# Longer runs a partition for x and the down weights, slots in 32 registers, and the second tile's A asked for earlier

## The chip, the cores and the metric

The kernel runs on one NeuronCore of a Trainium2 chip. The metric is the device time of one execution in microseconds, taken as the median of several runs. The core has a TensorE (PE, matmuls), a VectorE (DVE), a ScalarE (ACT), a GpSimd (POOL) and a SyncE (SP), which here does nothing but wait and issue DMAs; 16 DMA engines carry what is issued.

## What is computed

All matrices are float32. x has 128 sequences of 32 tokens of width 512 (4096 tokens). Two blocks with residuals follow each other:

```python
x = x + ffn0(cond0(x))        # L0
x = x + ffn1(cond1(x))        # L1
# cond0: x @ W + b + 2 * (x @ A[slot]) @ B[slot]      one of 32 adapters of rank 16 for each sequence
# ffn0:  (silu(x @ Wg.T) * (x @ Wu.T)) @ Wd.T         width 1376
# cond1: x @ W.T + 2 * sum over the top 2 of 8 experts, gates from a router with a language bias
# ffn1:  x @ Wb.T + b + 2 * sum over the top 2 of 8 experts, gates normalised
```

## The kernel before

The tokens are cut into NT = 8 tiles of 512. Everything on TensorE is done with each number split into a high and a low part of type float32r and three products (high by high, low by high, high by low).

**Stage 1** is cond0 and runs over the tiles. TensorE's work for a tile t is: the base product, 4 output blocks m by 4 chunks k by 3 products (48 matmuls of 512 columns); after m = 1 the product x A (`lora_in`, 24 matmuls of 256 columns, two groups g of 8 sequences); last the product with B (`cond_lora`, 24 matmuls of 256 columns), which closes the four banks. ACT copies a closed bank into `c_out` (L1005), SP stores it in `c_scratch` (L756). For tile 0 the loop over k is the outer one.

ACT and DVE make the high and the low parts: of x (L977, L1418), of A (`a_hi` L988, `a_lo` L1430), of B (L993, L1433), of the masked x A (`lora_in`: `h_masked` L1443, `lh_hi` L999, `lh_lo` L1449). Both run in program order: for tile 0 they turn A, split half of x of tile 1 (`split_x(1, (0, 1))`), and only then do `lora_in(0)`. In the tiles that follow: A and B of tile t, then x of t + 1, then `lora_in(t)`, then the closings.

Beside that, stage 1 prepares the down weights. `load_down` brings four row blocks (two pairs) into `wd_raw`, POOL makes four sums of each group (`down_sums`), ACT and DVE split seven operands of each group into a ring of four `dt` buffers (`down_hi`, `down_lo`, spread over the tiles by `d_due`), and SP stores each in `wd_scratch` (L623) and the last one in `ws_scratch` (L618). The buffers of the down weights lie where later the operands `cop` of stage 2 lie. So ACT's first `cop_split`, which stands ahead of the closings of tile 6, waits for the store of `ws_scratch` to have landed.

A is fetched by `gather_a`: slots are read from SBUF into SP's registers by one `reg_load` (L552, a TENSOR_LOAD of 16 registers), and each of the 16 sequences of a tile costs a register instruction (L557) and a DMA of 32 KB (L558). There is one `a_raw` buffer, so the gathers of tile t + 1 wait for `a_lo` of tile t, group by group. B's rows come by an indirect DMA on POOL.

All of these DMAs but B's are issued by SP in one order written out by hand in `sync_program`: at the start x and w0 of tile 0 in parts, `gather_a(0)`, x of tile 1 in two halves, `load_down(0)`, `load_down(1)`; then in each turn t the load of x of t + 2 (which waits until x of tile t is split), `gather_a(t + 1)`, and the stores of tile t with the stores of the down weights between them. In turn 5 the first load of c (`load_c(0, 0)`) comes behind the gathers, in turn 7 the second (`load_c(0, 1)`), for which `cop_begin(0, 1)` waits on DVE ahead of `lora_in(7)`.

**Stage 2** (ffn0) goes over pairs of tiles with a Strassen-like scheme of seven products. Its weights pass through a ring of 12 slots `wring`: for the first pair of tiles they are made on the spot and stored, later they are loaded (L603) from `wgu_scratch` and `wd_scratch`, each load issued as soon as the slot 12 places back is free. A down slot is 6 matmuls. **Stage 3** is the second block, with the weights of cond1 and ffn1 folded.

The layouts in DRAM: x is (tile, chunk, partition, token), so a tile's chunk is 2 KB a partition and the chunks lie 256 KB apart; `w_down` is plain rows of 2 KB; `wd_scratch` is (pair, product, partition, 512), `ws_scratch` is (half, partition, 512).

Of the kernel before, what the change touches and what calls it, by code (L numbers as in the profile page):

```python
# [3 lines left out]
F32 = mybir.dt.float32  # L4
# [6 lines left out]
P = 128  # L11
TOK = 512
LANG_BIAS = 5.0
SCALING = 2.0
DMA = 16
# [13 lines left out]
def build(nc, x, slots, slot_list, langs, w0, b0, a_cols, b_rows, w_gate, w_up, w_down, wb1, rhs2, ra1, b2t, b1, out):  # L29
    NT, KC, _, _ = x.shape  # L30
    D = KC * P
    NF = w_gate.shape[0]
# [223 lines left out]

    c_dram = nc.dram_tensor("c_scratch", list(x.shape), F32, kind="Internal").ap()
    t_dram = nc.dram_tensor("t_scratch", [NS, 4, 2, P, TOK], F32, kind="Internal").ap()
    x2_dram = nc.dram_tensor("x2_scratch", list(x.shape), F32, kind="Internal").ap()
# [123 lines left out]
    def x_parts(t):  # L383

        return [[0], [1], [2, 3]] if t == 0 else [[0, 1], [2, 3]]

# [152 lines left out]
    def sync_program(e):  # L539
        def load_x(t, ks):  # L540
            if ks[0] == 0 and t >= 2:
                e.wait_ge(x_lo, nth(t - 2))
            part = slice(ks[0], ks[-1] + 1)
            e.dma_start(x_raw[t % 2][:, part, :], x[t, part].rearrange("k p f -> p k f")).then_inc(  # L544
                x_in[t % 2][ks[0]], DMA)

        slot_regs = [e.alloc_register(f"slot{n}") for n in range(NG * GB)]

        def gather_a(t):

            first = t * NG * GB
            e.reg_load(slot_regs, slot_sb[0:1, first:first + NG * GB])  # L552
            for g in range(NG):
                if t > 0:
                    e.wait_ge(a_lo_done, NG * (t - 1) + g + 1)
                for b in range(GB):
                    slot = e.snap(slot_regs[g * GB + b], min_val=0, max_val=a_cols.shape[0] - 1)  # L557
                    e.dma_start(a_raw[:, g, b, :], a_cols[bass.ds(slot, 1)].rearrange("s p c -> (s p) c")).then_inc(  # L558
                        a_in[g], DMA)
# [28 lines left out]
        def load_slot(n):  # L588
# [12 lines left out]
            src = {"g": wgu_dram[a, b] if kind == "g" else None, "d": wd_dram[b, a] if kind == "d" else None,  # L601
                   "s": ws_dram[a] if kind == "s" else None}[kind]
            e.dma_start(plain(wring[n % N_W][:, :]), src).then_inc(w_moved[n % N_W], DMA)  # L603

        def load_down(g):
            if g >= 2:
                e.wait_ge(dt_lo_done, d_turn[g - 2, 3] + 1)
            if g < n_groups:
                n = pairs_of(g)
                src = w_down[4 * g * P:(4 * g + 2 * n) * P, :].rearrange("(r k p) d -> p r k d", r=n, k=2)  # L610
                e.dma_start(wd_raw[g % 2][:, 0:n, :, :], src).then_inc(wd_in[g % 2], DMA)  # L611
            else:
                e.dma_start(wd_raw[g % 2][:, 0, 0, :], w_down[2 * NP * P:NF * P, :]).then_inc(wd_in[g % 2], DMA)

        def store_down(n):
            e.wait_ge(dt_lo_done, n + 1)
            if n == len(d_steps):
                e.dma_start(ws_dram.rearrange("b p f -> p b f"),  # L618
                            plain(dt_[n % 4][:, :, :, :]).rearrange("p b h c -> p b (h c)")).then_inc(ws_stored, DMA)
                return  # L620
            g, i = d_steps[n]
            c = pairs_of(g)
            e.dma_start(wd_dram[2 * g:2 * g + c, i].rearrange("r p f -> p r f"),  # L623
                        plain(dt_[n % 4][:, 0:c, :, :]).rearrange("p r h c -> p r (h c)")).then_inc(dt_stored[n % 4], DMA)

        def extras(s, pos):
# [3 lines left out]
            if pos == slot_at["d", 1, 0]:  # L630
                for mp in range(2):
# [7 lines left out]
                    e.dma_start(res[mp][:, :], x[2 * s, mp]).then_inc(res_in[mp], DMA)  # L639
                    e.dma_start(res[2 + mp][:, :], x[2 * s, 2 + mp]).then_inc(res_in[2 + mp], DMA)  # L640
            if pos == slot_at["d", 1, 1] and s == NS - 1:
# [6 lines left out]
            if pos == slot_at["d", 6, 0]:  # L648
                e.wait_ge(h10_lo_done, 2 * s + 2)
                for mp in range(2):  # L650
                    e.dma_start(s1[mp][:, :], x[2 * s + 1, 2 + mp]).then_inc(x_second_in[mp], DMA)
                    e.dma_start(s2[mp][:, :], x[2 * s + 1, mp]).then_inc(x_second_in[mp], DMA)
            if pos == slot_at["d", 6, 3] and s + 1 < NS:
# [1590 lines left out]
```

## Time and profile before

| | |
|---|---|
| median of 3 runs | 1008.69 us (1008.25 to 1009.37) |
| profiled execution | 1007.51 us, span 1005.8 us |
| mean granted TensorE clock | 0.993 |
| busy: PE, DVE, ACT, POOL | 98%, 59%, 46%, 25% |
| bytes moved | 230.15 MB, 229 GB/s over the span |

The profile is that of one execution. An engine is busy when it works on an instruction; the issuing of DMAs is not counted, and stands under SPq. "Idle before <- X" names what released the engine. The granted clock is a share of full speed, so that 0.5 is the lower of TensorE's two levels (1.2 GHz) and 1.00 the higher (2.4 GHz).

### The profile page before, as it was taken

To read this page: it belongs to the slowest core of one execution; us is meant where nothing else is said; L and a number is where in the kernel's file an instruction comes from. 1 tells how busy PE (TensorE), PEld (TensorE's weight loads), DVE (VectorE), ACT (ScalarE), POOL (GpSimd) and SP (SyncE) were. 2 spreads that over 40 slices of the span, in tenths; PEclk is the share of its full clock that TensorE was granted. 3 is DMA by queue.
4 is the path that set the end of the run, shared out by engine and by line. 5 is a ranking of instruction groups with operands and counts; after the bars stand their busy time and mean duration, and the time that the engine had idled before them with its cause. 6 is when DMAs were issued, how large, how long until landed. Compare 5 with 4: busy or idle time off the path is not lost.

```text
span 1005.8 us, 14263 instructions
## 1 busy us (share of the span) xinstructions
PE 982.6 (98%) x4723; PEld 828.9 (82%) x4723; DVE 591.6 (59%) x969; ACT 465.0 (46%) x854; POOL 254.6 (25%) x244
## 2 busy tenths in 40 slices
PE   8989988999999999999999999999999999999998
PEld 7778876888888888888888888888888899898986
DVE  5555457667697342389243279533358588785862
ACT  4544555556483333375233367133347265445342
POOL 4232104454420441330171140062131280000000
PEclk9999999999999999999999999999999999999999
DMA  7888767677777986787887687797679660606132
GB/s 256 266 285 275 243 211 282 215 271 245 253 269 259 317 279 194 210 293 234 298 288 195 192 278 266 241 306 231 193 221 378 213 217 22 240 33 230 63 106 84
DMA packets 138515, 230.15 MB, mean 229 GB/s; under 512 B 30789, under 2 KB 30790, under 8 KB 138186
## 3 DMA queue, kind: packets, MB, share of 16 engines
q1 hardware_dynamic: 136928, 225.01, 67.5%
q0 software_dynamic: 1376, 4.22, 1.2%
q8 instruction: 39, 0.64, 0.3%
q14 instruction: 34, 0.28, 0.1%
q10 hardware_dynamic: 138, 0.01, 0.0%
HBM read 165.74 MB, written 63.44 MB: 228 GB/s over the span
## 4 chain that ended last, share of the span: by engine, by line
PE 83%; SPq 12%; issue 2%; DVE 2%; DMA 1%; ACT 0%; ACTq 0%; DVEq 0%
PE bank L1855 82%; SPq L558 5%; SPq L552 1%; SPq L623 1%; SPq L756 1%; SPq L544 1%; PE bank L2008 1%; SPq L557 1%; DMA c<-c_scratch 1%; DVE xa_lo L1418 0%; DMA a_raw<-in_a_cols 0%; DMA slot_i<-in_slots 0%; DVE b_lo L1433 0%; SPq L611 0%; DVE hg L1677 0%
## 5 line engine op out<-in xcount | busy, mean ns | idle before, releaser
L1855 PE MATMUL bank<-cop_hi,wring 128*128 128x512 f32 x1234 | 380.7, 389 | 0.1
L1855 PEld LDWEIGHTS bank<-cop_hi,wring 128*128 128x128 f32 x1234 | 231.6, 188 | 48.6 <-ACT bank L1073 0.4
L1855 PE MATMUL bank<-cop_lo,wring 128*128 128x512 f32 x616 | 239.6, 389 | 0.0
L1855 PE MATMUL bank<-op_hi,wring 128*128 128x512 f32 x560 | 173.7, 389 | 0.0
L1505 DVE TENSOR_TENSOR v<-bank,p7s 128x512 f32<-128x512 f32 x44 | 30.4, 692 | 203.5 <-PE bank L1855 203.5
L1855 PEld LDWEIGHTS bank<-cop_lo,wring 128*128 128x128 f32 x616 | 115.6, 188 | 23.9
L1855 PEld LDWEIGHTS bank<-op_hi,wring 128*128 128x128 f32 x560 | 105.1, 188 | 21.8
L1855 PE MATMUL bank<-op_lo,wring 128*128 128x512 f32 x280 | 108.9, 389 | 0.0
L1104 ACT ACTIVATE s<-bank 128x512 f32<-128x512 f32 x44 | 26.3, 598 | 118.8 <-PE bank L1855 118.6
L1491 DVE TENSOR_TENSOR op_lo<-h,op_hi 128x512 fp32r<-128x512 f32 x100 | 72.8, 746 | 3.3 <-ACT op_hi L1061 3.1
L1061 ACT ACTIVATE op_hi<-h 128x512 fp32r<-128x512 f32 x100 | 62.8, 628 | 13.7 <-PE bank L1855 12.8
L854 POOL TENSOR_TENSOR h_t<-h,h 128x512 f32<-128x512 f32 x20 | 26.3, 1317 | 161.4 <-DVE h L1527 161.4
L1073 ACT ACTIVATE bank<-bank 128x512 f32<-128x512 f32 x44 | 25.6, 582 | 78.6 <-PE bank L1855 78.6
L1855 PEld LDWEIGHTS bank<-op_lo,wring 128*128 128x128 f32 x280 | 52.6, 188 | 10.9
L1855 PE MATMUL bank<-xa_hi,w_hi 128*128 128x512 f32 x128 | 52.4, 409 | 4.6 <-ACT c_out L1005 3.7
L893 POOL TENSOR_TENSOR t_sum<-x_second,x_second 128x256 f32<-128x256 f32 x12 | 9.4, 817 | 177.0 <-DMA x_second<-x_scratch 177.0
L1855 PE MATMUL bank<-xa_lo,w_hi 128*128 128x512 f32 x128 | 51.7, 404 | 0.0
L1855 PE MATMUL bank<-xa_hi,w_lo 128*128 128x512 f32 x128 | 51.3, 401 | 0.0
L1510 DVE TENSOR_TENSOR p7s<-bank,p7s 128x512 f32<-128x512 f32 x44 | 30.4, 692 | 25.0 <-PE bank L1855 24.9
L809 POOL DMA_INDIRECT b_raw<-in_b_rows,row_i x16 | 19.0, 1187 | 90.5 <-DVE b_lo L1433 84.1
L1080 ACT ACTIVATE p7s<-bank 128x512 f32<-128x512 f32 x44 | 26.3, 598 | 30.6 <-PE bank L1855 30.6
L1095 ACT ACTIVATE s<-bank 128x512 f32<-128x512 f32 x44 | 26.3, 598 | 30.6 <-PE bank L1855 30.6
(225 smaller groups left out, 1930.5 us busy)
## 6 DMA issues: line engine op xcount, KB each, us to landing
wring<-wgu_scratch SPq DMA_DIRECT2D x231, 256.0 KB, 3.0
wring<-wd_scratch SPq DMA_DIRECT2D x140, 256.0 KB, 4.9
wgu_scratch<-wring SPq DMA_DIRECT2D x77, 256.0 KB, 3.5
c_scratch<-c_out SPq DMA_DIRECT2D x32, 256.0 KB
c<-c_scratch SPq DMA_DIRECT2D x32, 256.0 KB, 3.2
xs_raw<-x_scratch SPq DMA_DIRECT2D x16, 512.0 KB, 5.8
out<-res SPq DMA_DIRECT2D x32, 256.0 KB, 2.1
x_raw<-in_x SPq DMA_DIRECT2D x15, 512.0 KB, 6.6
```

The source lines that it names most:

```text
L558: e.dma_start(a_raw[:, g, b, :], a_cols[bass.ds(slot, 1)].rearrange("s p c -> (s p) c")).then_inc(a_in[g], DMA)
L809: e.indirect_dma_start(out=b_raw[g][:, :], out_offset=None, in_=b_rows, in_offset=bass.IndirectOffsetOnAxis(ap=row_i[:, col:col + 1], axis=0),
L854: e.tensor_tensor(h_t3[p][:, :], h22[p][:, :], h12[p][:, :], ALU.subtract).then_inc(t3_done, 1)
L1061: e.activation(op_hi[n % N_OP][:, :], op_source[i][p][:, :], ACT.Copy).then_inc(op_hi_done, 1)
L1073: e.activation(bank_y[b][:, :], bank_a[b][:, :], ACT.Copy).then_inc(ay_done, 1)
L1080: e.activation(p7s[b][:, :], bank_w[b][:, :], ACT.Copy).then_inc(p7s_done, 1)
L1095: e.activation(s1[j % 2][:, :], bank_a[j % 2][:, :], ACT.Silu).then_inc(silu1_done, 1)
L1104: e.activation(s2[j % 2][:, :], bank_z[j % 2][:, :], ACT.Silu).then_inc(silu2_done, 1)
L1491: e.tensor_tensor(op_lo[n % N_OP][:, :], op_source[i][p][:, :], plain(op_hi[n % N_OP][:, :]), ALU.subtract).then_inc(op_lo_done, 1)
L1505: e.tensor_tensor(v[b][:, :], bank_z[b][:, :], p7s[b][:, :], ALU.add).then_inc(gc22_done, 1)
L1510: e.tensor_tensor(p7s[b][:, :], bank_y[b][:, :], p7s[b][:, :], ALU.add).then_inc(gc21_done, 1)
L1855: return e.matmul(out_ap, lhs, rhs, start=start, stop=stop, skip_group_check=True)
```

## The change

Three things are changed, all of them on the side of the DMAs; TensorE, VectorE, ScalarE and GpSimd run the same instructions in the same order.

1. **Layouts.** x becomes (tile, partition, chunk, token), so a whole tile is 8 KB a partition in one run. A tile's load is one DMA of 1 MB for t > 0 (`x_parts`), where there were two of 512 KB; for tile 0 the parts stay, and the last of them has a run of 4 KB. A user of one chunk of x now reads runs of 2 KB that lie 8 KB apart. The down weights are laid out by partition, so that the load of a group has a run of 8 KB (4 KB for the last pair). `wd_scratch` is (group, product, partition, pair, 512): a store writes runs of 4 KB, and a ring slot's load reads runs of 2 KB that lie 4 KB apart. `ws_scratch` likewise.
2. **Slots.** `reg_load` reads 32 registers for two tiles at even t and nothing at odd t.
3. **Order.** `gather_a(1)` is asked for ahead of `load_down(1)` and the load of x of tile 2.

```diff
-    NT, KC, _, _ = x.shape
+    NT, _, KC, _ = x.shape
...
-    wd_dram = nc.dram_tensor("wd_scratch", [NP, 8, P, 4 * P], F32, kind="Internal").ap()
-    ws_dram = nc.dram_tensor("ws_scratch", [2, P, 4 * P], F32, kind="Internal").ap()
+    wd_dram = nc.dram_tensor("wd_scratch", [(NP + 1) // 2, 8, P, 2, 4 * P], F32, kind="Internal").ap()
+    ws_dram = nc.dram_tensor("ws_scratch", [P, 2, 4 * P], F32, kind="Internal").ap()
...
-        return [[0], [1], [2, 3]] if t == 0 else [[0, 1], [2, 3]]
+        return [[0], [1], [2, 3]] if t == 0 else [[0, 1, 2, 3]]
...
-            e.dma_start(x_raw[t % 2][:, part, :], x[t, part].rearrange("k p f -> p k f")).then_inc(
-                x_in[t % 2][ks[0]], DMA)
+            e.dma_start(x_raw[t % 2][:, part, :], x[t][:, part, :]).then_inc(x_in[t % 2][ks[0]], DMA)
...
-        slot_regs = [e.alloc_register(f"slot{n}") for n in range(NG * GB)]
+        slot_regs = [e.alloc_register(f"slot{n}") for n in range(2 * NG * GB)]
...
-            first = t * NG * GB
-            e.reg_load(slot_regs, slot_sb[0:1, first:first + NG * GB])
+            n = NG * GB
+            if t % 2 == 0:
+                e.reg_load(slot_regs, slot_sb[0:1, t * n:(t + 2) * n])
...
-                src = w_down[4 * g * P:(4 * g + 2 * n) * P, :].rearrange("(r k p) d -> p r k d", r=n, k=2)
+                src = w_down[:, 4 * g:4 * g + 2 * n, :].rearrange("p (r k) d -> p r k d", r=n)
...
         load_down(0)
-        load_down(1)
         for t in range(NT):
+            if t == 0:
+                gather_a(t + 1)
+                load_down(1)
             if t + 2 < NT:
                 for ks in x_parts(t + 2):
                     load_x(t + 2, ks)
-            if t + 1 < NT:
+            if 0 < t < NT - 1:
                 gather_a(t + 1)
```

The change on SP, behind the last gather of tile 0. `x_raw_75` is the buffer of tile 1's x, `x_raw_74` that of tile 0 and then 2. Before:

```order
L558 DMA a_raw<-in_a_cols 128x64
L544 DMA x_raw_75<-in_x 128x2x512 x2
L611 DMA wd_raw_76<-in_w_down 128x4x512
L611 DMA wd_raw_77<-in_w_down 128x4x512
L544 DMA x_raw_74<-in_x 128x2x512 x2
L552 TENSOR_LOAD slot_sb
L557 ISA
L558 DMA a_raw<-in_a_cols 128x64
```

Now, with the middle of the 16 gathers of tile 1 left out:

```order
L559 DMA a_raw<-in_a_cols 128x64
L545 DMA x_raw_75<-in_x 128x2048
L612 DMA wd_raw_76<-in_w_down 128x2048
L558 ISA
L559 DMA a_raw<-in_a_cols 128x64
...
L559 DMA a_raw<-in_a_cols 128x64
L612 DMA wd_raw_77<-in_w_down 128x2048
L545 DMA x_raw_74<-in_x 128x2048
L759 DMA c_scratch<-c_out_50 128x512
```

The gathers of tile 1 have moved ahead of the second group of down weights and of tile 2's x, their TENSOR_LOAD is gone, and each tile of x is one DMA.

The change on SP between the stores of tile 1 and the gathers of tile 3, where `dt` are the split down weights. Before:

```order
L623 DMA wd_scratch<-dt_83 128x2x512
L756 DMA c_scratch<-c_out_53 128x512
L623 DMA wd_scratch<-dt_84 128x2x512
L611 DMA wd_raw_76<-in_w_down 128x2x512
L544 DMA x_raw_74<-in_x 128x2x512 x2
L552 TENSOR_LOAD slot_sb
L557 ISA
L558 DMA a_raw<-in_a_cols 128x64
```

Now:

```order
L624 DMA wd_scratch<-dt_83 128x1024
L759 DMA c_scratch<-c_out_53 128x512
L624 DMA wd_scratch<-dt_84 128x1024
L612 DMA wd_raw_76<-in_w_down 128x1024
L545 DMA x_raw_74<-in_x 128x2048
L558 ISA
L559 DMA a_raw<-in_a_cols 128x64
```

The stores and loads are the same in number but for x, with longer runs, and the TENSOR_LOAD is there in every second turn only.

## Rows read from the trace of the kernel before

**Rows 1.** Windows: busy us of each engine, granted clock, DMA share, GB/s
```profile
0.00:171.00 171.00, 151.42 (x789) 129.43 (x789) 95.32 (x138) 84.28 (x155) 50.21 (x56) 0.96 0.78 260
171.00:1006.00 835.00, 831.14 (x3935) 699.45 (x3934) 496.23 (x832) 380.75 (x700) 204.42 (x188) 1.00 0.67 222
```

**Rows 2.** Waits of PE, 20 to 172 us: total us, times, longest
```profile
PE bank L1855 <- DVE a_lo L1430: 6.8, 5, 2.2
PE bank L1855 <- DVE lh_lo L1449: 6.0, 3, 4.6
PE bank L1855 <- ACT c_out L1005: 3.7, 1, 3.7
```

**Rows 3.** Timeline of PE: start us, us, form, idle before and its releaser
```profile
22.88 0.39 PE L1855 MATMUL bank<-lh_hi,b_hi 128*128 128x256 f32 x1 [0.45 <-DVE lh_lo L1449]
...
25.85 0.40 PE L1855 MATMUL bank<-xa_hi,w_hi 128*128 128x512 f32 x1
...
33.60 0.39 PE L1855 MATMUL bank<-xa_hi,a_hi 128*128 128x256 f32 x1 [2.12 <-DVE a_lo L1430]
...
122.74 0.40 PE L1855 MATMUL bank<-xa_hi,w_hi 128*128 128x512 f32 x1
...
139.54 0.28 PE L1855 MATMUL bank<-lh_hi,b_lo 128*128 128x256 f32 x1
...
168.23 0.39 PE L1855 MATMUL bank<-cop_hi,wring 128*128 128x512 f32 x1
```

**Rows 4.** Windows behind two long waits of PE, columns as in rows 1
```profile
34.00:37.50 3.50, 3.50 (x19) 3.50 (x19) 3.12 (x6) 3.47 (x7) 1.24 (x2) 0.53 1.02 382
...
163.70:167.20 3.50, 3.43 (x16) 3.43 (x17) 3.29 (x6) 3.02 (x6) 1.15 (x2) 0.53 0.30 114
```

**Rows 5.** Timeline of SP: start us, us spent issuing, count
```profile
14.65 0.94 SPq L544 DMA_DIRECT2D x_raw<-in_x  x2
15.63 1.02 SPq L611 DMA_DIRECT2D wd_raw<-in_w_down  x2
16.70 1.98 SPq L544 DMA_DIRECT2D x_raw<-in_x  x2
19.88 12.07 SPq L558 DMA_DIRECT2D a_raw<-in_a_cols  x16
...
41.33 9.12 SPq L558 DMA_DIRECT2D a_raw<-in_a_cols  x16
...
138.78 8.57 SPq L558 DMA_DIRECT2D a_raw<-in_a_cols  x16
```

**Rows 6.** The loads of the slots: count, ns min/median/max, first and last start
```profile
L552 SPq TENSOR_LOAD <-slot_sb x8: 985/1547/3057, 5.0 to 135.5; - x8
```

**Rows 7.** A piece of the chain that ended last: start us, us
```profile
154.57 5.55 DMA c<-c_scratch
```

**Rows 8.** Windows: two neighbouring stretches of stage 1
```profile
52.00:66.00 14.00, 13.07 (x81) 11.47 (x80) 9.71 (x12) 7.87 (x15) 7.97 (x6) 1.00 1.02 367
66.00:72.00 6.00, 5.62 (x30) 4.41 (x28) 1.84 (x3) 1.47 (x3) 0.00 (x0) 1.00 0.33 74
```

**Rows 9.** Window of stage 2 in which rhs2 and wb1 (runs of 10 KB) land
```profile
755.00:760.00 5.00, 5.00 (x24) 4.14 (x23) 5.00 (x6) 2.98 (x6) 2.16 (x2) 1.00 1.01 422
```

**Rows 10.** Timeline of ACT: two idle times and what ended them
```profile
18.87 1.16 ACT L977 ACTIVATE xa_hi<-x_raw 128x512 fp32r<-128x512 f32 x2 [1.11 <-DMA x_raw<-in_x]
...
140.74 1.67 ACT L1046 ACTIVATE cop_hi<-c 128x512 fp32r<-128x512 f32 x3 [6.09 <-DMA ws_scratch<-dt]
```

**Rows 11.** DMA issues of the whole span: count, KB each, median us to landing
```profile
wring<-wd_scratch SPq DMA_DIRECT2D x140, 256.0 KB, 4.9
...
a_raw<-in_a_cols SPq DMA_DIRECT2D x128, 32.0 KB, 2.0
...
x_raw<-in_x SPq DMA_DIRECT2D x2, 256.0 KB, 3.7
w_raw<-in_w SPq DMA_DIRECT2D x2, 256.0 KB, 4.2
```

More of the change, by code:

```diff
@@ L255, in build @@
     bank_a, bank_y, bank_w, bank_z = (banks[i::4] for i in range(4))
-    c_dram = nc.dram_tensor("c_scratch", list(x.shape), F32, kind="Internal").ap()
+    c_dram = nc.dram_tensor("c_scratch", [NT, KC, P, TOK], F32, kind="Internal").ap()
     t_dram = nc.dram_tensor("t_scratch", [NS, 4, 2, P, TOK], F32, kind="Internal").ap()
-    x2_dram = nc.dram_tensor("x2_scratch", list(x.shape), F32, kind="Internal").ap()
+    x2_dram = nc.dram_tensor("x2_scratch", [NT, KC, P, TOK], F32, kind="Internal").ap()
     wgu_dram = nc.dram_tensor("wgu_scratch", [NF, 8, P, 4 * P], F32, kind="Internal").ap()
-    wd_dram = nc.dram_tensor("wd_scratch", [NP, 8, P, 4 * P], F32, kind="Internal").ap()
-    ws_dram = nc.dram_tensor("ws_scratch", [2, P, 4 * P], F32, kind="Internal").ap()
+    wd_dram = nc.dram_tensor("wd_scratch", [(NP + 1) // 2, 8, P, 2, 4 * P], F32, kind="Internal").ap()
+    ws_dram = nc.dram_tensor("ws_scratch", [P, 2, 4 * P], F32, kind="Internal").ap()
     sem = nc.alloc_semaphore
@@ L556, in gather_a @@
                 for b in range(GB):
-                    slot = e.snap(slot_regs[g * GB + b], min_val=0, max_val=a_cols.shape[0] - 1)
+                    slot = e.snap(slot_regs[(t % 2) * n + g * GB + b], min_val=0, max_val=a_cols.shape[0] - 1)
                     e.dma_start(a_raw[:, g, b, :], a_cols[bass.ds(slot, 1)].rearrange("s p c -> (s p) c")).then_inc(
@@ L600, in load_slot @@
                     e.wait_ge(w_moved[k % N_W], DMA * w_moves(k))
-            src = {"g": wgu_dram[a, b] if kind == "g" else None, "d": wd_dram[b, a] if kind == "d" else None,
-                   "s": ws_dram[a] if kind == "s" else None}[kind]
+            src = {"g": wgu_dram[a, b] if kind == "g" else None, "d": wd_dram[b // 2, a][:, b % 2, :] if kind == "d" else None,
+                   "s": ws_dram[:, a, :] if kind == "s" else None}[kind]
             e.dma_start(plain(wring[n % N_W][:, :]), src).then_inc(w_moved[n % N_W], DMA)
@@ L609, in load_down @@
                 n = pairs_of(g)
-                src = w_down[4 * g * P:(4 * g + 2 * n) * P, :].rearrange("(r k p) d -> p r k d", r=n, k=2)
+                src = w_down[:, 4 * g:4 * g + 2 * n, :].rearrange("p (r k) d -> p r k d", r=n)
                 e.dma_start(wd_raw[g % 2][:, 0:n, :, :], src).then_inc(wd_in[g % 2], DMA)
             else:
-                e.dma_start(wd_raw[g % 2][:, 0, 0, :], w_down[2 * NP * P:NF * P, :]).then_inc(wd_in[g % 2], DMA)
+                e.dma_start(wd_raw[g % 2][:, 0, 0, :], w_down[:, 2 * NP, :]).then_inc(wd_in[g % 2], DMA)
         def store_down(n):
@@ L617, in store_down @@
             if n == len(d_steps):
-                e.dma_start(ws_dram.rearrange("b p f -> p b f"),
+                e.dma_start(ws_dram,
                             plain(dt_[n % 4][:, :, :, :]).rearrange("p b h c -> p b (h c)")).then_inc(ws_stored, DMA)
@@ L622, in store_down @@
             c = pairs_of(g)
[L623 removed]
+            e.dma_start(wd_dram[g, i][:, 0:c, :],
                         plain(dt_[n % 4][:, 0:c, :, :]).rearrange("p r h c -> p r (h c)")).then_inc(dt_stored[n % 4], DMA)
@@ L638, in extras @@
                         e.wait_ge(pair_sum_done, PIECES * 4 * s)
-                    e.dma_start(res[mp][:, :], x[2 * s, mp]).then_inc(res_in[mp], DMA)
-                    e.dma_start(res[2 + mp][:, :], x[2 * s, 2 + mp]).then_inc(res_in[2 + mp], DMA)
+                    e.dma_start(res[mp][:, :], x[2 * s][:, mp, :]).then_inc(res_in[mp], DMA)
+                    e.dma_start(res[2 + mp][:, :], x[2 * s][:, 2 + mp, :]).then_inc(res_in[2 + mp], DMA)
             if pos == slot_at["d", 1, 1] and s == NS - 1:
@@ L650, in extras @@
                 for mp in range(2):
-                    e.dma_start(s1[mp][:, :], x[2 * s + 1, 2 + mp]).then_inc(x_second_in[mp], DMA)
-                    e.dma_start(s2[mp][:, :], x[2 * s + 1, mp]).then_inc(x_second_in[mp], DMA)
+                    e.dma_start(s1[mp][:, :], x[2 * s + 1][:, 2 + mp, :]).then_inc(x_second_in[mp], DMA)
+                    e.dma_start(s2[mp][:, :], x[2 * s + 1][:, mp, :]).then_inc(x_second_in[mp], DMA)
             if pos == slot_at["d", 6, 3] and s + 1 < NS:
@@ L2214 @@
     arrays = {
-        "x": x.reshape(n_tiles, TOK, D // P, P).transpose(0, 2, 3, 1),
+        "x": x.reshape(n_tiles, TOK, D // P, P).transpose(0, 3, 2, 1),
         "slots": np.asarray(itok_B_0_23).reshape(-1, P // 16).T,
@@ L2226 @@
         "w_up": by_chunk(padded(L0_ffn_W_up)),
-        "w_down": padded(np.asarray(L0_ffn_W_down).T),
+        "w_down": chunked(padded(np.asarray(L0_ffn_W_down).T)),
         "wb1": by_part(np.concatenate([np.asarray(L1_cond_W), B1.transpose(1, 0, 2).reshape(D, -1)], axis=1)),
```

## The prediction

> **What bounds the kernel now.** I looked first at where TensorE stands still. Cut at 171 us [rows 1], the span splits into two different kernels. After it TensorE is busy 831.1 of 835 us at a granted clock of 1.00, and what is idle lies at the very end; there it is the bound, and its instructions aren't touched. Before it, 19.6 of 171 us are idle and the clock is 0.96. So all that this change can win lies in stage 1, and the rest of the span, 834.6 us, is a constant as long as its loads stay hidden.
>
> The list of PE's waits names three causes in stage 1 [rows 2]: A's low part (6.8 us in 5 waits), the low part of x A (6.0 us in 3, the longest 4.6) and a closed bank (3.7 us). Each leads back to SP:
> - A is late since its gathers are issued late. The 16 of tile 1 begin at 19.88, behind both groups of down weights and tile 2's x, and take 12.07 us where the last tile's take 8.57 [rows 5]: the queue is full. TensorE waits 2.12 us at 33.60 [rows 3].
> - The closed bank waits for ACT, which stood 6.09 us until the last store of the down weights had landed at 140.74 [rows 10].
> - The wait of 4.6 us goes back to the load of c, 5.55 us in the chain behind its issue at 154.57 [rows 7].
>
> SP's turn is too long. From the gathers of tile 2 at 41.33 to those of tile 7 at 138.78 it makes five turns [rows 5], 19.5 us each. TensorE needs less: tile 6, which has no wait, begins at 122.74 and its last matmul at 139.54 [rows 3], so a tile is 16.9 us.
>
> The waits cost more than their idle time. Behind the one at 33.60 and the longest one the granted clock is 0.53 for 3.5 us [rows 4], the lower level (1.2 GHz) after the engine had stood for 2 us and more. Each costs 3.5 x 0.47 = 1.65 us; there are four such stretches.
>
> **What can be won.** Tile 1 begins at 25.85 and stage 2 at 168.23 [rows 3]. Seven tiles of 16.9 us would be 118.3, so 142.4 - 118.3 = **24.1 us** is the pool. The parts agree: 6.8 + 6.0 + 3.7 less the 0.45 in tile 0 is 16.1, the clock 6.6, the rest is the drain of the pipeline before each wait.
>
> **The change part by part.**
>
> *The order.* Ahead of tile 1's gathers now stand one load of x and one of the down weights: 14.65 + 0.47 + 0.5 = 15.6 [rows 5]. Their own condition (A of tile 0 split) falls at about the same time. 16 gathers at the last tile's pace are 8.6 us, so they end near 24.7 instead of 31.95, and A is there, 2.0 us later [rows 11], before TensorE wants it (25.85 and a third of a tile, 31.3). The wait of 2.12 us and its clock go. Queued behind them are the second group of down weights, not used before tile 2, and tile 2's x. Its 2 MB in front and itself land some 6 us after 24.7 at 367 GB/s [rows 8], by 31.5; ACT asks for it behind A and B of tile 1, about then. I cost that at nothing; if it is late, what shows it is x, not A. The stores of tile 0 follow, and the gathers of tile 2 begin near 24.7 + (41.33 - 31.95) + 0.9 for the load moved in = 35.0 instead of 41.33.
>
> *x in one piece.* It saves one issue a turn: 0.47 in an empty queue, 0.99 in a full one [rows 5], I take 0.7. In tile 0 it costs. ACT splits half of tile 1's x ahead of `lora_in(0)`, and waited for that half until 18.87 [rows 10], 4.2 us after its issue. The whole has 512 KB more: 1.4 us at 367 GB/s, 1.2 at the 422 that the runs of 10 KB reach [rows 8, 9]. TensorE already waited 0.45 at 22.88 for what comes of it [rows 3], so all of it lands on the path: **+1.3** (1.0 to 2.4, the last if it shares the engines with the megabyte behind it).
>
> *The slots.* A load of 16 registers takes 985 ns at best, 1547 in the median, 3057 at worst [rows 6]. One of 32 isn't in the trace: it costs nothing more if it is all latency, 1.0 more if it is all registers; I take **+0.5**, the middle, since the row can't part the two. The first one stands ahead of tile 0's gathers and so of tile 1's x: it is on the path. Later two turns save a load of 1.5 and pay 0.5: 0.5 a turn. The Trainium skill (DMA: Bandwidth & Descriptors, Latency and other measured facts) gives such a load a floor of about 600 ns; by that the 16 registers are the other 0.4, the first load would cost 0.4 more and not 0.5, and the sum would move by 0.1.
>
> *Longer runs.* A turn carries some 14 x 367 + 6 x 74 GB/s, 5.6 MB [rows 8]; the engines are full for 14 us and nearly empty while SP issues gathers. With 422 in place of 367 for the parts with long runs (over half) 1 us of back-pressure goes; nothing, if the queue's room counts bytes. I take 0.5. The kernel needs 5.6 MB in 16.9 us, 331 GB/s: it fits, but with little to spare.
>
> *SP's turn* is then 19.5 - 0.7 - 0.5 - 0.5 = 17.8 (17.3 to 18.3), 0.9 longer than TensorE's. It starts with a lead: A of tile 2 is there at 35.0 + 9.1 + 2.0 + 1.3 (its split) = 47.4, wanted at 27.65 + 16.9 + 5.5 = 50.0, 2.6 us later. Five turns lose 4.5. So near the end A, or the down weights' last store and the load of c that hang on the same turn, are late by **2.0** (0 at 17.3; 4.4 at 18.3).
>
> *The clock.* The wait at 22.88 becomes 0.45 + 1.3 + 0.5 = 2.25, as long as one behind which the clock fell. I count one stretch, **+1.65** (0 to 3.3).
>
> *Ring loads from `wd_scratch`* in runs of 2 KB at 4 KB apart: 140 of them [rows 11], each issued 12 slots ahead, 12 x 6 matmuls x 0.23 = 16 us, against 4.9 us to landing. Nearest rows: w0's parts come in such runs, 8 KB apart, and land in 4.2 us where x's, contiguous, take 3.7. Nothing, while that cover stands.
>
> **The sum**, against the profiled execution of 1007.5 us: -24.1 + 1.3 + 0.5 + 2.0 + 1.65 = -18.65, so 988.9. The median of the runs lies 1.2 above the profiled one: **990**.
>
> **The rivals.**
> - *The engines, not SP, set the turn.* In the full stretches of 14 us SP's issues are held up whatever it issues, and a dropped TENSOR_LOAD only moves gathers into the jam. For it: a load of 3057 ns beside a median of 1547. Against: 6 us a turn in which the engines are a third busy. SP's turn would shrink by the spared x issue alone, to 18.9; five turns lose 10, 7 beyond the lead, with two or three stretches of low clock instead of one: 24.1 - 1.8 - 7.4 - 4.1 = 10.8 won, 998.
> - *All of the pool.* Turn 17.3 or less, no clock lost at 22.88: 24.1 - 1.8 = 22.3 won, 986, or 984 with the cheap ends of both costs.
> - *It doesn't do what it says.* A of tile 1 is asked sooner, but 16 small DMAs behind 2 MB land no sooner, and SP then stands for the stores: 2.12 + 1.65 saved at most, 1.8 paid, some 2 for the dropped issues: 1005.
> - *Slower.* The place is the down products: 4 passes of 35 slots read `wd_scratch`. If half-used rows of 4 KB made such a load twice as dear, 0.7 us of all engines (256 KB at 367) would be 1.4, more than the 1.37 us in which TensorE uses up a slot, and with the other traffic some 0.4 us a slot would be missing: 140 x 0.4 = 56 us, 1045. It decides from about 1.0 us a load. Against it stand w0's rows. [...]
>
> **How the numbers follow.** The forecast (984 to 993) gets 0.50, the engines' rival (993 to 1001) 0.24, all of the pool and below 984 0.09, "not what it says" (1001 to 1006) 0.06, no change 0.04, slower 0.07. From 982 to 1000 about 0.8 is held. Within 0.2% (2 us, about what a measurement of this kernel can tell) 0.04, faster 0.89, slower 0.07.
>
> **What would show it.** Tile 1 begins near 27.6, with a wait of 2.2 us for `lh_lo` ahead of tile 0's B product. The wait for `a_lo` in tile 1 is gone. SP's gathers of tile 2 begin near 35, and its turns last 17.8 us or wait for ACT. Stage 2 begins near 149.5, with the span behind it 834 to 835 us. A 32-register load takes 1.5 to 2.1 us in the median. Wrong would be: a wait for `x_raw` on ACT in tile 1 or 2, turns of 19 us, a wait of TensorE for a ring slot after stage 1, or a load from `wd_scratch` that lands in over 8 us.

## The result, and the profile after

Over ten runs of each the kernel takes **1005.89 us** after the change (1004.41 to 1006.97) and 1009.06 before (1006.85 to 1011.86): a ratio of **0.9968** (95% interval 0.9957 to 0.9979), 3.2 us faster where 18.7 were forecast. The profiled execution has a span of 1003.9 us.

Windows of the changed kernel, in stage 1 and behind it (columns as in rows 1), then its waits of PE from 20 to 172 us (total us, times, longest), which answer to [rows 1, 2]:

```profile
0.00:171.00 171.00, 150.77 (x801) 128.66 (x802) 99.86 (x147) 86.72 (x163) 50.78 (x56) 0.97 0.78 262
171.00:1003.00 832.00, 828.91 (x3924) 697.45 (x3922) 491.82 (x823) 377.88 (x692) 204.38 (x188) 1.00 0.67 223
```

```profile
PE bank L1858 <- DVE lh_lo L1452: 5.4, 3, 2.4
PE bank L1858 <- ACT c_out L1008: 4.2, 1, 4.2
PE bank L1858 <- DVE a_lo L1433: 3.4, 4, 2.3
PE bank L1858 <- issue: 1.8, 3, 0.7
```

After 171 us little has changed: TensorE is idle for 3.1 us of 832, at a granted clock of 1.00. One of its weight loads stands 0.5 us for a ring slot, whose load from `wd_scratch`, issued at 749.87, landed after 12.46 us. The gain lies in stage 1. Stage 2 begins 4.3 us sooner, and 3.7 of them are busy time: up to there the same 777 matmuls keep TensorE busy for 144.96 us instead of 148.65, at a mean granted clock of 0.97 instead of 0.96, while its idle time falls by 0.6 only. The span shrinks by just 1.9 us, since 1.3 of the rest stand in two short idle times of TensorE at 166.07 and 168.36 (releaser "issue"), which the first profile of the kernel before lacks and its second (e12, below) has. Most of what was to be won still stands: the closed bank's wait is 4.2 us, no shorter than before, and `a_lo` has 3.4 instead of 6.8. TensorE's timeline in the changed kernel (start us, us, form, idle before and its releaser), to be laid beside [rows 3]:

```profile
9.52 0.75 PE L1858 MATMUL bank<-xa_hi,w_hi 128*128 128x512 f32 x1 [3.78 <-DVE w_lo L1425]
...
27.77 0.39 PE L1858 MATMUL bank<-lh_hi,b_hi 128*128 128x256 f32 x1 [2.12 <-DVE lh_lo L1452]
...
30.75 0.40 PE L1858 MATMUL bank<-xa_hi,w_hi 128*128 128x512 f32 x1
...
47.43 0.40 PE L1858 MATMUL bank<-xa_hi,w_hi 128*128 128x512 f32 x1
...
93.50 0.39 PE L1858 MATMUL bank<-xa_hi,a_hi 128*128 128x256 f32 x1 [2.26 <-DVE a_lo L1433]
...
143.02 0.79 PE L1858 MATMUL bank<-xa_hi,w_hi 128*128 128x512 f32 x1 [4.22 <-ACT c_out L1008]
...
160.93 0.39 PE L1858 MATMUL bank<-lh_hi,b_hi 128*128 128x256 f32 x1 [2.39 <-DVE lh_lo L1452]
...
163.91 0.40 PE L1858 MATMUL bank<-cop_hi,wring 128*128 128x512 f32 x1
```

Tile 1 (30.75 to 47.43) is now free of waits and takes 16.7 us instead of 20.6; the wait of 2.12 us for `a_lo` at 33.60 is gone. The `lh_lo` wait in tile 0 is 2.12 us (2.25 forecast). But tile 1 begins 3.1 us later than forecast, and stage 2 at 163.91, not near 149.5.

SP shows why. Its timeline in the changed kernel (start us, us spent issuing, count), beside [rows 5]; L759 is the store of `c_out`, L619 that of `ws_scratch`, L587 the last load of c:

```profile
19.53 8.81 SPq L559 DMA_DIRECT2D a_raw<-in_a_cols  x16
28.38 0.43 SPq L612 DMA_DIRECT2D wd_raw<-in_w_down  x1
28.86 0.44 SPq L545 DMA_DIRECT2D x_raw<-in_x  x1
29.59 0.97 SPq L759 DMA_DIRECT2D c_scratch<-c_out  x2
...
36.27 0.67 SPq L545 DMA_DIRECT2D x_raw<-in_x  x1
43.51 8.88 SPq L559 DMA_DIRECT2D a_raw<-in_a_cols  x16
...
133.27 0.96 SPq L619 DMA_DIRECT2D ws_scratch<-dt  x1
134.42 9.54 SPq L559 DMA_DIRECT2D a_raw<-in_a_cols  x16
...
151.24 0.43 SPq L587 DMA_DIRECT2D c<-c_scratch  x1
```

The gathers of tile 1 do go quicker (8.81 us instead of 12.07). Yet those of tile 2 begin at 43.51, later than before (41.33), not at 35.0. Between 36.94 and 43.5 stands the load of slots, which the chain of what ended last holds twice in this stretch of the kernel (start us, us), with the group of the four loads (ns, min/median/max) under it; [rows 6] are those of before:

```profile
7.86 2.07 SPq L553
...
36.98 6.35 SPq L553
```

```profile
L553 SPq TENSOR_LOAD <-slot_sb x4: 2072/3096/6353, 7.9 to 113.9; - x4
```

One load of 32 registers costs 2.07 us at 7.86 and 6.35 us at 36.98. In this stretch the DMA engines are full: windows of the changed kernel, columns as in rows 1.

```profile
36.00:40.00 4.00, 4.00 (x30) 3.81 (x29) 1.53 (x3) 1.77 (x4) 2.12 (x2) 1.00 1.01 403
40.00:44.00 4.00, 4.00 (x19) 3.31 (x18) 2.69 (x5) 1.06 (x2) 0.00 (x0) 1.00 1.04 421
```

The 2 MB that the new order puts behind the gathers of tile 1 (28.38, 28.86) meet the stores of tile 0 and tile 3's x.

Full engines alone don't make such a load dear, though. Loads of 16 registers took 0.98 us at 18.72 in the kernel before, with the DMA share at 1.06 and 410 GB/s, and 3.06 us at 135.54, with 1.04 and 402 GB/s; the first load of 32 took 2.07 us in e4 at 416 GB/s as well. What else must come together is not shown. Nor is 6.35 us the rule: at the same place, in the same order, e13 has 4.63 us and e17 4.99.

### The profile page after: what moved, and what is told of

It is laid out like the page before. It is cut to its first block, busy times and chain, and to the rows that moved or that the text cites. A ratio compares the mean times of both kernels' runs of the same rounds, so it can differ in the third digit from the quotient of the medians.

```text
span 1003.9 us, 14252 instructions
## 1 busy us (share of the span) xinstructions
PE 979.7 (98%) x4723; PEld 826.1 (82%) x4723; DVE 591.7 (59%) x969; ACT 464.6 (46%) x854; POOL 255.2 (25%) x244
## 4 chain that ended last, share of the span: by engine, by line
PE 81%; SPq 9%; DMA 3%; DVE 3%; issue 2%; ACT 1%; ACTq 0%; DVEq 0%
PE bank L1858 81%; SPq L559 4%; SPq L553 1%; DMA wring<-wd_scratch 1%; DVE xa_lo L1421 1%; SPq L759 1%; SPq L624 1%; PE bank L2011 1%; DMA slot_i<-in_slots 1%; DMA c<-c_scratch 1%; DMA a_raw<-in_a_cols 0%; SPq L558 0%; DMA x_raw<-in_x 0%; DVE b_lo L1436 0%; SPq L545 0%
## 5 line engine op out<-in xcount | busy, mean ns | idle before, releaser
L1513 DVE TENSOR_TENSOR p7s<-bank,p7s 128x512 f32<-128x512 f32 x44 | 30.4, 691 | 24.8 <-PE bank L1858 24.7
```

Source lines behind the costliest of these rows:

```text
L1513: e.tensor_tensor(p7s[b][:, :], bank_y[b][:, :], p7s[b][:, :], ALU.add).then_inc(gc21_done, 1)
```

## The experiments

Sixteen kernels were run, each beside the kernel before on the same chip, and the kernel before was profiled once more (e12). Ratios are to the kernel before (95% interval); 0.001 is 1.0 us. "Gathers 7" is when SP's gathers of tile 7 begin, from each one's profile. Each differs in one or two edits from a named kernel.

| | ratio | median us | gathers 7 | stage 2 begins |
|---|---|---|---|---|
| before, profiled again (e12) | 1 | | 139.79 | 166.79 |
| changed kernel | 0.9968 (0.9957 to 0.9979) | 1005.9 | 134.42 | 163.91 |
| e1: slots by 16 | 0.9960 (0.9948 to 0.9972) | 1005.6 | 138.53 | 168.62 |
| e2: before, new order | 0.9981 (0.9971 to 0.9991) | 1007.8 | 139.43 | 169.87 |
| e3: before, new layouts | 0.9975 (0.9964 to 0.9985) | 1006.6 | 137.07 | 165.68 |
| e4: x in its old layout | 0.9947 (0.9934 to 0.9960) | 1003.8 | 132.76 | 161.65 |
| e5: slots early | 0.9927 (0.9913 to 0.9940) | 1001.3 | 131.16 | 159.72 |
| e6: e5, x old, tile 1's in halves | 0.9933 (0.9919 to 0.9946) | 1002.9 | 134.39 | 162.91 |
| e7: down weights in old layouts | 0.9978 (0.9966 to 0.9991) | 1007.0 | 136.00 | 165.71 |
| e8: changed kernel, old order | 0.9965 (0.9951 to 0.9978) | 1005.7 | 135.64 | 164.16 |
| e9: e5, x in its old layout | 0.9928 (0.9910 to 0.9946) | 1002.7 | 133.44 | 163.24 |
| e10: e9, second down load late | 0.9918 (0.9900 to 0.9936) | 1001.2 | 130.12 | 158.48 |
| e11: e9, first load of c late | 0.9923 (0.9902 to 0.9945) | 1001.4 | 132.35 | 162.10 |
| e13: changed, 22 splits in 5 tiles | 0.9948 (0.9934 to 0.9963) | 1004.7 | 135.76 | 163.97 |
| e14: e5, 22 splits in 5 tiles | 0.9924 (0.9895 to 0.9953) | 1002.1 | 131.94 | 162.56 |
| e15: before, 22 splits in 5 tiles | 0.9996 (0.9982 to 1.0009) | 1009.1 | 139.23 | 168.29 |
| e16: e5, one split a closing | 0.9938 (0.9921 to 0.9955) | 1002.7 | 130.96 | 161.87 |
| e17: changed, one split a closing | 0.9964 (0.9950 to 0.9978) | 1005.8 | 136.63 | 168.60 |

### The parts of the change

**Slots by 16**, in the changed kernel:

```diff
-            if t % 2 == 0:
-                e.reg_load(slot_regs, slot_sb[0:1, t * n:(t + 2) * n])
+            e.reg_load(slot_regs[(t % 2) * n:(t % 2 + 1) * n], slot_sb[0:1, t * n:(t + 1) * n])
```

> The changed kernel with 16 registers loaded for each tile instead of 32 for two. Theory A (a load of slots is paid by the register, and dearer the fuller the DMA engines are, so the 32-register load of 6.35 us ahead of tile 2's gathers ate what the new order had won): the first load takes about 1.1 us instead of 2.07, the one ahead of tile 2's gathers about 3 instead of 6.35, gathers of tile 2 begin near 40 instead of 43.51, and the kernel gains 2 to 4 us on the changed one (1002 to 1004). Rival B (the engines set the turn, and the load only stands where the queue would stand anyway): the gathers behind are held up instead and the time is that of the changed kernel within 1 us.

No clear difference in sum (0.9960 against 0.9968, the intervals overlap). The first load costs 1.18 us instead of 2.07, the one ahead of tile 2's gathers 3.37 instead of 6.35, and these begin at 39.62, 3.9 us sooner; but then they take 11.74 us instead of 8.88. Of the 3.9 us saved ahead of the gathers 2.9 were paid in them, and there is a load in every turn again.

**The order alone** on the kernel before, and **the layouts alone** (with x in one DMA and 16 registers); their edits are those pieces of the diff above.

> The kernel before with the new order alone: old layouts, x in two halves, 16 registers. Theory A: the order is what helps; the wait for a_lo in tile 1 (2.12 us and its slow clock) goes, tile 0 stays as before (first real matmul at 6.66), 2 to 5 us faster than before. Rival C (the layouts are what helped, the order is neutral since SP then stands for the stores): within 1 us of the kernel before.

> The kernel before with the new layouts and x in one DMA, old order, 16 registers. Theory D (x in runs that lie 8 KB apart lands later in tile 0): the first real matmul starts near 9 us instead of 6.66, as in the changed kernel, and the kernel is 1 to 3 us slower than before in tile 0; later turns of SP are shorter by 0.7 to 1 us each. Rival E (the late start of the changed kernel is a matter of one execution, or of the registers): first real matmul at 6.6 to 7, and the kernel 1 to 4 us faster than before.

The order alone takes away the wait for `a_lo` in tile 1 and wins 1.9 us of 1009; its gathers of tile 2 begin at 41.63, no sooner than before. The layouts alone win 2.5. **The changed kernel with the old order** is as fast as with the new one:

> The changed kernel with the old order at the start (both groups of down weights and tile 2's x ahead of tile 1's gathers). If the new order only moves 2 MB from a stretch in which SP issues gathers into the one in which SP wants to store, TensorE waits 2 us for a_lo in tile 1 again but the gathers of tile 2 begin at 41 to 43 as in the changed kernel: 1005 to 1007.5. If the order is worth its 3.8 us (wait and slow clock), 1009 to 1010.

0.9965 against 0.9968. So the order, for which I had counted most of the gain, is worth nothing in this company. The wait in tile 1 is no sign of its worth either: in e3 and e8, with the old order, tile 1 has no wait for `a_lo` and takes 16.8 and 16.9 us, since TensorE comes to it only at 30.18 and 31.36, not at 25.85 as in the profile from which I predicted. What hid A's lateness there was a late tile 0.

**The down weights' layouts undone** (`w_down`, `wd_scratch`, `ws_scratch`) and **x's undone** (the declaration, and its four uses, as here):

```diff
-            e.dma_start(x_raw[t % 2][:, part, :], x[t][:, part, :]).then_inc(x_in[t % 2][ks[0]], DMA)
+            e.dma_start(x_raw[t % 2][:, part, :], x[t, part].rearrange("k p f -> p k f")).then_inc(x_in[t % 2][ks[0]], DMA)
```

> The changed kernel with the down weights, wd_scratch and ws_scratch in their old layouts. If the longer runs of the stores shorten SP's turns, they are 18.8 to 19.5 us instead of 18.2 and the time is 1007 to 1009; if they do nothing, or the half rows that the ring loads read cost what they win (5.5 us to landing instead of 4.9), the time is 1005 to 1006.5.

> The changed kernel with x in its old layout, each tile still one DMA, now in runs of 2 KB. Theory D: the first real matmul is back at 6.6 to 7 us and the kernel gains 2 to 3 us on the changed one. Rival E: first real matmul as in the changed kernel or of either kind, time within 1 us; if the runs of 8 KB had shortened SP's turns, it is slower by 1 to 3 us.

The first is 1 us slower than the changed kernel, the second 2.1 us faster; both intervals touch the changed kernel's, and on top of early slots (e9 against e5) x's old layout made no difference. What x's layout is worth in sum stays open. Its place in tile 0 is seen in the profiles, though. The gathers and VectorE's first split both stand behind an 8-KB load of slot numbers, issued at 1.39 while x and w0 come in. Its piece of the chain in the kernel before, in its second profile, and in the changed kernel, in this order:

```profile
1.39 3.60 DMA slot_i<-in_slots
```

```profile
1.38 5.85 DMA slot_i<-in_slots
```

```profile
1.39 6.46 DMA slot_i<-in_slots
```

In nine profiles with x in its old layout TensorE's first base product of tile 0 begins at 6.66 to 9.51, in the median 8.59; in ten with the new one at 8.75 to 10.66, in the median 10.05. So chunks of 2 KB at 8 KB apart go with a start about 1.5 us later, though the two groups overlap; and the profile from which I predicted had the quickest start of all 19.

### Where the slots are loaded

e5: each tile's 16 slots are loaded right behind the gathers of the tile before, when the engines are nearly empty, and not ahead of the gathers that use them.

```diff
+        def load_slots(t):
+            n = NG * GB
+            e.reg_load(slot_regs[(t % 2) * n:(t % 2 + 1) * n], slot_sb[0:1, t * n:(t + 1) * n])
...
+            if 0 < t < NT - 1:
+                load_slots(t + 1)
```

> The changed kernel with each tile's 16 slots loaded right behind the gathers of the tile before, where the DMA engines are nearly empty, instead of 32 right ahead of the gathers. Theory A (a register costs a read through the queues that the DMAs fill): the loads take 1.0 to 1.3 us each instead of 2.1 to 6.4, SP has 5 to 8 us more over stage 1, the gathers of tile 2 begin near 38 instead of 43.5, stage 2 begins 3 to 6 us sooner: 1000 to 1003. Rival B (the engines set the turn, and whatever SP saves it stands for later): the loads are short but the stores and gathers behind them are held up, the time is 1004.5 to 1006.5.

This is the one clear gain: 1001.34 us, 4.5 better than the changed kernel by the medians and 4.1 by the ratios, the intervals apart. The edit changes both the number of registers and the place; e1, which has the number alone, gained next to nothing, and e5 is 3.3 us better than e1 by the ratios (intervals apart), so it is the place. The group of its loads, and its gathers of tile 2 on SP:

```profile
L551 SPq TENSOR_LOAD <-slot_sb x8: 971/976/1167, 8.1 to 121.3; - x8
```

```profile
35.68 13.38 SPq L561 DMA_DIRECT2D a_raw<-in_a_cols  x16
```

A load costs 0.97 to 1.17 us, and the gathers of tile 2 begin at 35.68, as the prediction had them (35.0). But they take 13.38 us in the full engines, not 9, and end at 49.06 against 52.39. So the head start was there to be had, and a good half of it is lost again in these gathers. The 3.3 us left at their end are still there at the gathers of tile 7 (131.16 against 134.42).

**x's old layout and halves on top** (e6), **x's old layout alone on top** (e9):

> The run before (slots early) with x in its old layout, and tile 1's x in two halves again. If x in one DMA is what makes TensorE wait 2.1 to 2.5 us ahead of tile 0's B product, that wait is back at about 0.5, and the kernel gains 2 to 3 us on the changed kernel with x in its old layout (1003.8), with the early slots 4 to 7: 997 to 1000. If engines set the turn, 1002 to 1004.

> The changed kernel with two edits that each won alone: the 16 slots of a tile are loaded behind the gathers of the tile before (1001.3 us, 4.5 better than the changed kernel), and x keeps its old layout, one DMA a tile (1003.8, 2.1 better). If the two costs are separate terms, as I hold, they add up: 1005.9 - 4.5 - 2.1 = 999.3 us, first matmul of tile 0 before 9.0, stage 2 at 158 to 159. Rival: both only take slack out of the same turn, and the next limit (the last store of the down weights, which ACT awaits) stands: 1001 to 1002, no better than the slots alone.

In e6, with halves, there is no `lh_lo` wait in tile 0, but in e5, with x in one DMA, it was 0.2 us already (1.33 in e9); one of 2.52 us stands in tile 1 instead; 1002.9. e9 missed its 999.3 by 3.4: the gains don't add up.

**The second group of down weights behind the gathers of tile 2** (e10, on e9):

```diff
             if t == 0:
                 gather_a(t + 1)
-                load_down(1)
...
+            if t == 1:
+                load_down(1)
```

> The kernel of e9_early_xold with the load of the second group of down weights (1 MB) issued behind the gathers of tile 2 instead of behind those of tile 1; it isn't used before tile 2. Theory that the 2 MB which the changed order puts behind the gathers of tile 1 fill the DMA engines from 32 to 46 us, and that this is what holds up the gathers of tile 2: these take 8.8 to 10.5 us instead of the 13.4 to 15.4 of the two runs with early slots, tile 2's x is there 1 to 2 us sooner, and the time is 0 to 1.5 us below e9_early_xold. Rival: the gathers of tile 2 are slow because they come while A's buffer is waited for or because of tile 0's stores and tile 3's x alone: they still take over 12 us, and the time stays or gets worse, since the megabyte now lies in tile 1's stores.

```profile
34.75 11.41 SPq L561 DMA_DIRECT2D a_raw<-in_a_cols  x16
```

The gathers of tile 2 take 11.41 us instead of the 14.86 of e9, more than the 8.8 to 10.5 expected, and those of tile 3 in turn 11.62 instead of 9.27. The megabyte did hold them up, but not alone: the windows from 36 to 44 still carry 417 and 409 GB/s. It has the lowest ratio of all, not told apart from e5 and e9.

### What sets the end of stage 1

The prediction had the last two waits, for the closed bank and for the load of c, go with SP's shorter turns. They stood in every profile. e12 is the kernel before a second time; e11 (on e9) puts `load_c(0, 0)` behind tile 5's stores.

> The kernel before, profiled a second time, for what differs between two executions of one kernel. The first matmul of tile 0's low part waited 0.9 us and ended its wait at 6.66 in the profile of before, but the two kernels with the old layout of x had it at 8.7 and those with the new one at 9.5 to 10.4. If the 6.66 is a lucky execution, this one has it near 8.7 and the new layout costs tile 0 about 1 us; if it is the old load of 16 slots and the old code that give it, it is 6.7 again and the changed kernel loses 3 us in tile 0. Stage 2 begins at 168 to 170.

> The kernel of e9_early_xold with the first load of c (1 MB in four DMAs) issued behind tile 5's stores instead of ahead of them. ACT waits for the store of ws_scratch until 136.2 and TensorE 4.7 us for what comes of it. If SP's queue in front of that store is what counts, it is issued near 127.8 instead of 129.7, lands 2 to 3 us sooner, the wait of TensorE for the closed bank falls to 2 to 3 us, and the time is 1.5 to 3 us below e9_early_xold. Rival: the same ACT instruction needs c too, which now lands some 7 us behind its issue near 130, so at 137: the releaser becomes c, nothing won or 1 us lost.

In e11 the store of `ws_scratch` is issued at 127.98 instead of 132.41, but ACT now waits for c until 137.07: the rival was right. Three kernels then spread the split steps of the down weights over five tiles instead of six:

```diff
-    d_points = 4 * (NT - 2)
+    d_points = 4 * (NT - 3)
```

> The changed kernel with the 22 split steps of the down weights spread over five tiles instead of six (d_points is 4 x 5), so that the store of ws_scratch, which ACT awaits ahead of the closings of tile 6, is issued a turn sooner. In the changed kernel tiles 6 and 7 take 42.3 us where 33.4 would do, behind the closed bank (4.2) and the load of c that follows from it (2.4). Theory 1, these two waits hang on this one chain (gathers of tile 6, loads of c, eight stores, landing of ws_scratch) and not on how long SP's turns are: ACT then waits for nothing or for c until about 133, the bank's wait falls below 1, tiles 6 and 7 take 34 to 37 us, and the time is 5 to 8 us below 1005.9, 998 to 1001, less what the fuller turns 1 to 4 lose. Theory 2, as my prediction had it, the waits come of SP's turns: another store or load of c is late in its place and the turns, fuller by a fifth of the down weights' stores, get longer: at best 1004, or slower than 1006.

> The same edit, five tiles instead of six, on the changed kernel with each tile's 16 slots loaded behind the gathers of the tile before (1001.3 us). Theory 1: tiles 6 and 7 from 42.2 to 34 to 37 us, and 994 to 997 in all, since both gains lie in different tiles. Theory 2: with SP's turns already relieved the fuller turns cost what the end gains: 1000 to 1003.

> The same edit alone on the kernel before. By theory 1 its last two tiles have the same chain (42.6 and 45.5 us in its two profiles): they take 35 to 38 us and the time is 1001 to 1004. By theory 2 the turns of 19.5 us only get longer: no gain, 1008 or more.

The bank's wait is gone in all three and tiles 6 and 7 take 35.5, 36.0 and 35.5 us instead of 42.3 in the changed kernel. Yet e13 wins about 2 us (0.9948 against 0.9968, the intervals just overlap), the others nothing: tile 3 takes 24 to 26 us. ACT in e14:

```profile
76.20 0.63 ACT L1041 ACTIVATE dt<-ds 128x512 fp32r<-128x512 f32 x1 [6.45 <-DMA wd_scratch<-dt]
```

A turn with five steps meets four `dt` buffers; the fifth waits 6.45 us for a store, ahead of A's split. So I gave each closing one step, at most four a turn:

```diff
-        return range(n * q // d_points, n * (q + 1) // d_points) if q < d_points else range(0)
+        return range(q, q + 1) if q < n else range(0)
```

> The kernel with early slots (1001.3 us), with one split step of the down weights at each of the first 22 closings: four a tile in tiles 0 to 4, the last two at the first two closings of tile 5. With five tiles (e14_both) the fifth step of a turn stood on ACT for a dt buffer, 5.9 us in tile 3; four steps a turn meet four buffers. The store of ws_scratch is then the fourth store of tile 5 and not the eighth, issued near 126.5 instead of 129.7. Theory 1 (one fixed chain to the closed bank): it lands 3 us sooner, the bank's wait falls from 4.7 to 1 to 2, tile 3 keeps 17 to 19 us, tiles 6 and 7 take 38 to 39 us instead of 42.2, 997 to 998.5 in all. Theory 2 (a gain at the end is paid in the fuller turns whatever their form): 1001 to 1003.

> The same edit on the changed kernel (1005.9 us), whose slots are still loaded 32 at a time. Theory 1: the bank's wait falls from 4.2 to about 1, no step waits for a dt buffer, 1002 to 1003.5. Theory 2: no gain, 1004.5 to 1007.

Nothing is won. TensorE's two waits in e5, then in e16:

```profile
139.02 0.80 PE L1864 MATMUL bank<-xa_hi,w_hi 128*128 128x512 f32 x1 [4.66 <-ACT c_out L1014]
...
156.75 0.38 PE L1864 MATMUL bank<-lh_hi,b_hi 128*128 128x256 f32 x1 [2.29 <-DVE lh_lo L1458]
```

```profile
137.60 0.50 PE L1864 MATMUL bank<-xa_hi,w_hi 128*128 128x512 f32 x1 [1.79 <-ACT c_out L1014]
...
157.00 0.58 PE L1864 MATMUL bank<-lh_hi,b_hi 128*128 128x256 f32 x1 [5.33 <-DVE lh_lo L1458]
```

The first wait shrinks by 2.9 us and the second grows by 3.0; in e17 likewise, 6.9 us in sum against 6.6. Both are views of one thing: SP reaches its last load of c at 148.02 in e16 and 147.01 in e5, behind the gathers of tile 7 (130.96 and 131.16), the loads of gate and up and four stores. TensorE, sooner at one gate, waits longer at the next. "Theory 1" falls. The table shows it over all 19 profiles: from the gathers of tile 7 to stage 2 it is 27.0 to 32.0 us, in the median 29.5, with or without the bank's wait. So the tail hangs on SP's order of issues. SP is not alone on the chain, though. It waits itself in the changed kernel from 20 to 172 us, 7.0 us for `c_out` of ACT and 2.5 for `dt` of DVE. And between 18.44 and 34.03 the chain that ended last runs over the landing of tile 1's x (4.84 us) and DVE's splits, back to a store of `dt`; in the kernel before it ran over the gathers of tile 1. How much of a turn is SP's own issuing and how much these waits no run here parts.

## Why the prediction was wrong

The direction was right and the size six times too large. In SP's terms the prediction reads: gathers of tile 2 at 35.0, five turns of 17.8, so those of tile 7 at 124.0, and stage 2 25.5 us later, 149.5. Measured are 43.51, five turns of 18.2 (134.42) and 29.5, so 163.91. The 14.4 us between are 8.5 + 1.9 + 4.0, and each has its step. (Behind stage 2's start the changed kernel's profile has 840.0 us and that of the kernel before 837.6; these 2.4 us are beyond the prediction's steps, and 1.3 of them are the two short idle times named above.)

- **The head start, 8.5 us.** Two things. Everything of tile 0 ran later, so the gathers of tile 1 ended at 28.34, not 24.7: 3.6 us. The slot numbers landed 2.9 us later (6.46 us behind their issue, not 3.60), partly by x's layout and partly because the profile read had an unusually early one, and the first wide load took 0.9 us more than the 1.18 of the narrow one, not 0.5. The other 4.9 us is, but for 0.3, the second load of 32 registers, 6.35 us where the kernel before had 1.76. I took +0.5 for a load between 985 and 1985 ns, although [rows 6] had one of 16 at 3057 already: I asked whether the price is latency or registers, and not what the engines do at its place. It cost 6.35 us. In e5, with the load moved to an emptier place, the gathers began at 35.68.
- **"I cost that at nothing."** This is the sentence behind the head start that failed. The megabytes moved behind the gathers of tile 1 were costed by when their user needs them, not by the queue behind them. ACT did wait 3.24 us for tile 2's x, but TensorE had no wait in tile 1 and its next was 0.68 us, at 55.17; what counted is what SP had to issue from 36 to 44 us, when the engines were full. Where no wide load stood there, the gathers themselves were held up (11.4 to 15.5 us in e1, e5, e6, e9, e10, e11, e14 and e16).
- **The turn, 1.9 us.** 18.2 instead of 17.8, inside the stated 17.3 to 18.3. The early start that should have hidden the difference to TensorE's 16.7 was not there. And the agreement is partly luck: where the head start was there (e5), five turns took 19.1 us each with the held-up gathers of tile 2 in them, above the range and near the 18.9 of the rival that the engines set them.
- **The end, 4.0 us.** The pool of 24.1 took all waits from 25.85 to 168.23 for removable. The last two are the same chain's tail: the gathers of tile 7, then the loads and stores up to the last load of c, then its landing. The prediction shortened the turns up to tile 7 and let the tail's waits vanish, where it should have carried the sum on to that load (29.5 us in [rows 3, 5]: 168.23 - 138.78). The second profile of the kernel before has 27.0, so single profiles tell this to some 2 us only.

The wait for `lh_lo` in tile 0 was forecast as 2.25 us and measured as 2.12. That too is partly luck: the kernels with the new order and x in one DMA show 0.2 us (e5) to 3.03 us (e7) there.

The clock's term was in the wrong place. I counted one stretch of 1.65 us behind the wait in tile 0. Windows of the changed kernel behind three of its four waits of over 2 us (27.77, 93.50, 143.02), columns as in rows 1:

```profile
28.00:31.50 3.50, 3.50 (x28) 3.37 (x28) 3.50 (x3) 2.62 (x5) 3.50 (x3) 1.00 0.81 212
...
94.00:97.50 3.50, 3.50 (x17) 3.02 (x16) 3.50 (x6) 1.85 (x4) 2.84 (x3) 0.62 1.01 347
143.00:146.50 3.50, 3.48 (x9) 2.79 (x10) 3.15 (x6) 3.50 (x7) 0.00 (x0) 0.56 0.57 146
```

Behind the first the granted clock stayed at 1.00, the higher level; behind the other two it is 0.62 and 0.56 of full speed, so for most of these stretches it was at the lower one. Behind the fourth wait (2.39 us, 160.93) it stayed at 1.00 too. Reckoned as the prediction did, this costs 3.5 x 0.38 and 3.5 x 0.44, 2.9 us in sum. The four stretches of the kernel before, which the prediction took at 0.53 each and 6.6 us, have 0.53, 0.67, 0.53 and 0.53 (from 34.00, 73.94, 143.55 and 163.70), 6.1 us. So some 3 us of low clock are gone, about as much as the kernel gained. A wait of about 2 us does not always bring the lower level: of five of 2.1 to 2.4 us in the two profiles three did and two did not.

Of the rivals, "it doesn't do what it says" (1005) came nearest, and for its reason: SP stands for the stores and loads, and what the order wins at A goes there. But it had 0.06. "The engines set the turn" (998) was right that issues are held up whatever they are, and wrong that only the turns suffer. The slower case was refuted by the time. The loads from `wd_scratch` land in 5.5 us in the median (before 4.9, [rows 11]), and TensorE's matmuls wait for none; but the layout isn't shown to be the cause, since the second profile of the kernel before, e7 with the old layout and e4 with the new one all have 5.2. One of the prediction's signs of being wrong did show, the load that landed after 12.46 us, at a cost of 0.5 us of a weight load.

The Trainium skill (DMA: Bandwidth & Descriptors, Latency and other measured facts) gives a register load a floor of about 600 ns. The prediction read that as a fixed part beside the registers, and the runs here don't bear this reading out: at the same place, the first load, 16 registers took 1.18 us and 32 took 2.07, which makes 56 ns a register and 0.3 us beside it, an estimate from two points. A load of few registers was not run, so the floor itself stays untested.

Not settled: why a TENSOR_LOAD is dear in some places and not in others with engines as full; how much of SP's turn is its own; what x's new layout is worth in sum; and the share of the down weights' layouts, about 1 us by e7 and not told from nothing.

## What to carry to other kernels

- Where one queue issues everything, follow its chain from the first instruction to the last that the next stage waits for, and carry every saving on to that point. TensorE's idle time by cause is not the pool: two waits on one chain trade places (4.7 + 2.3 became 1.8 + 5.3).
- What is moved behind an urgent transfer is not free because its user comes late. Ask which issues stand behind it while the engines are full; and put an instruction that reads memory into registers where they are nearly empty. That was worth 4.5 us against the changed kernel and 3.3 against e1, which differs from e5 in the place alone; the whole change was worth 3.2.
- Profile the kernel before twice. Its start differed by 2.25 us between two executions whose totals differ by 0.14, and in the one that started later stage 2 began 1.4 us sooner. A difference of 1 or 2 us at one point of two single profiles tells little.

## What the chip showed that I had not expected

- A load of slots into registers costs 0.97 us for 16 and 2.07 for 32 at the quickest (as the first load of the kernel 1.18 and 2.07), which is close to proportional to the number, and up to 3.4 and 6.35 us while the engines run at 400 GB/s. Other loads were as quick as the quickest beside 410 GB/s. In the first place two loads of 16 would be little dearer than one of 32 (2 x 1.18 against 2.07).
- An 8-KB load issued at 1.39 us, while x and w0 come in, landed after 3.6 to 7.6 us in the profiles here; a small transfer can take as long as a large one beside it (tile 0's parts of 256 KB took 3.7 and 4.2 us in [rows 11]), and the first split and matmul wait for it.
- Longer runs showed no shorter landing where the same bytes can be compared: the stores of `dt` take 6.0 us in the median in runs of 4 KB in the changed kernel (4.4 in e8, 6.5 in e4), and in runs of 2 KB 5.5 before (6.0 in e7, 7.0 in e2).
